# Edge counts built over 160 buckets of 16 nodes instead of 80 buckets of 32 nodes

## The reference, cut to what matters

```
x = x + L0_gnn(layernorm(x))     # twice: xW = x @ W[r]; agg = segment_sum(xW[edge_type, src], dst)
x = x + L0_ffn(layernorm(x))     # top 2 of 8 experts
x = x + L1_gnn(layernorm(x))     # three times: msg = h[src] * norm; agg = segment_sum(msg, dst)
x = x + L1_ffn(layernorm(x))     # top 2 of 8 experts
```

## Time and profile before

| | |
|---|---|
| median of three runs | 2288.94 us (2286.91 to 2291.53) |
| the profiled execution | 2287.31 us, its span 2285.4 us |
| busy, share of the span | PE 83%, DVE 53%, ACT 44%, POOL 41% |
| mean granted TensorE clock | 0.914 |
| first to last gather of `aggregate_and_gate` | 636.2 to 1075.6 us |
| last count product, last sum added | 1032.0 us, 1091.0 us |

### The profile page before, as it was taken

The page is one execution under the profiler, slowest core; times in us unless marked ns, Lnnn a source line. Parts: engine busy times, 40 slices in busy tenths (PEclk is TensorE's granted clock), DMA queues, the critical chain, the costliest instruction groups (busy, mean ns, idle before and its releaser), DMA issues. The chain is left out here.

```text
span 2285.4 us, 37277 instructions
## 1 busy us (share of the span) xinstructions
PE 1888.0 (83%) x10428; PEld 1570.3 (69%) x10428; DVE 1210.0 (53%) x2759; ACT 1002.6 (44%) x2229; POOL 934.0 (41%) x877
## 2 busy tenths in 40 slices
PE   5995688778848888787499999679899864999997
PEld 3873576656735555555489999558788854899996
DVE  6331222212268898793655555365554566666664
ACT  1555456546455656555033333245444421233332
POOL 0115777777367777776033433220000000333332
PEclk9997889989979999998599999879999965999998
DMA  4894666665368655564545342237664456424262
GB/s 153 344 363 175 223 219 213 226 224 207 127 206 320 215 199 193 197 206 150 207 124 160 90 123 42 63 133 251 235 218 173 166 223 248 121 42 123 43 191 41
DMA packets 127195, 410.00 MB, mean 179 GB/s; under 512 B 21012, under 2 KB 60928, under 8 KB 108544
## 3 DMA queue, kind: packets, MB, share of 16 engines
q1 hardware_dynamic: 56848, 185.62, 22.2%
q0 software_dynamic: 48096, 106.74, 18.2%
q10 hardware_dynamic: 22032, 114.96, 13.2%
HBM read 256.77 MB, written 150.47 MB: 178 GB/s over the span
## 5 line engine op out<-in xcount | busy, mean ns | idle before, releaser
L2231 PE MATMUL ps<-ring,halves 128*128 x3384 | 579.6, 326 | 11.8 <-SPq L2193 4.2
L2231 PEld LDWEIGHTS ps<-ring,halves 128*128 128x128 f32 x3384 | 487.2, 192 | 54.1 <-issue 13.5
L1429 POOL DMA_INDIRECT ring<-tab_rel_next,gidx_relation x313 | 345.2, 1103 | 137.6 <-issue 94.8
L1111 POOL DMA_INDIRECT relation_rest<-tab_rel,gidx_relation x313 | 309.9, 990 | 105.5 <-issue 94.8
L2340 ACT ACTIVATE x_all<-ps 128x512 f32<-128x512 f32 x188 | 113.0, 601 | 453.0 <-PE ps L2250 448.8
L1186 PE MATMUL ps<-relation_rest,slots 128*128 x784 | 210.5, 415 | 105.0 <-SPq L1026 103.7
L1521 PE MATMUL ps<-ring,slots 128*128 x784 | 205.2, 410 | 87.8 <-SPq L1306 46.3
L1888 PE MATMUL ps<-node_rows,blocks 128*128 128x512 f32 (+1 forms) x1200 | 258.8, 366 | 0.3 <-ACT blocks L1770 0.3
L1186 PEld LDWEIGHTS ps<-relation_rest,slots 128*128 128x128 f32 x784 | 157.8, 207 | 144.5 <-issue 119.3
L1521 PEld LDWEIGHTS ps<-ring,slots 128*128 128x128 f32 x784 | 151.1, 202 | 128.6 <-issue 108.3
L1888 PEld LDWEIGHTS ps<-node_rows,blocks 128*128 128x128 f32 x1200 | 203.3, 194 | 31.2 <-ACT blocks L1770 0.8
(11 more groups left out here) (281 smaller groups left out, 2773.9 us busy)
## 6 DMA issues: line engine op xcount, KB each, us to landing
ring<-split_weights SPq DMA_DIRECT2D x12, 4096.0 KB, 14.5
split_weights<-relation_rest ACTq DMA_DIRECT2D x32, 1024.0 KB, 7.4
slots<-tab_counts SPq DMA_DIRECT2D x40, 640.0 KB, 4.0
tab_rel<-relation_rest SPq DMA_DIRECT2D x20, 1024.0 KB, 5.8
tab_rel_next<-relation_rest ACTq DMA_DIRECT2D x20, 1024.0 KB, 4.2
relation_rest<-in_ffn_units ACTq DMA_DIRECT2D x16, 1024.0 KB, 5.5
ring<-split_weights SPq DMA_DIRECT2D x8, 2048.0 KB, 22.9
split_weights<-ring ACTq DMA_DIRECT2D x16, 1024.0 KB
```

The source lines that it names most:

```text
L1111: nc.gpsimd.indirect_dma_start(rows[:, s * wide:s * wide + D], None, table, bass.IndirectOffsetOnAxis(ap=gidx[:, t:t + 1], axis=0)).then_i ...
L1429: nc.gpsimd.indirect_dma_start(rows[:, s * D:(s + 1) * D], None, table, bass.IndirectOffsetOnAxis(ap=gidx[:, t:t + 1], axis=0)).then_inc(g ...
L2231: ins = nc.tensor.matmul(to, lhs[left], weights(slot, right, at, n), start=first and (left, right) == (0, 0), stop=last and left == 1)
```

## The change

Buckets are 16 nodes wide, so there are 160. Each takes four edge tiles, 20 x 16 = 320 places and so one PSUM bank: four buckets are in flight in the four banks. `pair_hots` has eight buffers, four for even and four for odd buckets, and the wait ahead of each is replaced by the one wait ahead of `src_hots` (for the bucket before last). `count_full` counts buckets, not edge tiles. All three engines do two buckets behind each of the first 80 groups. DVE makes two buckets ahead of the loop instead of one. Four small tensors used after the counts (`token_of_slot`, `place_of_slot`, `weight_of_slot`, `w_comb`) now lie within `count_key`, which is no longer needed then.

```
-NARROW = 32
+NARROW = 16
-WINDOW = 6
+WINDOW = 4
-HOTS = WINDOW
+HOTS = 2 * WINDOW
+COUNTBANKS = 4
...
-                step(v.tensor_single_scalar(part, raw[0], 5, ALU.arith_shift_right))
+                step(v.tensor_single_scalar(part, raw[0], 4, ALU.arith_shift_right))
...
-                    act.wait_ge(count_full, (k + 1) * WINDOW)
+                    act.wait_ge(count_full, k + 1)
...
-                    for g in range(2):
-                        to = strips[b % 2][:, g * (NPAD // 2):(g + 1) * (NPAD // 2)].rearrange("p (g c) -> p g c", c=P)
-                        nc.scalar.activation(to[:, :, q * NARROW:(q + 1) * NARROW],
-                                             self.ps[BANKS + k % 2 * 2 + g][:, 0:half].rearrange("p (g c) -> p g c", c=NARROW),
-                                             ACT.Copy).then_inc(bank_out, 1)
+                    to = strips[b % 2].rearrange("p (g c) -> p g c", c=P)
+                    nc.scalar.activation(to[:, :, q * NARROW:(q + 1) * NARROW],
+                                         self.ps[BANKS + k % COUNTBANKS][:, 0:KEYS].rearrange("p (g c) -> p g c", c=NARROW),
+                                         ACT.Copy).then_inc(bank_out, 1)
...
                     if k >= 2:
-                        dve.wait_ge(count_full, (k - 1) * WINDOW)
+                        dve.wait_ge(count_full, k - 1)
...
                     for j in range(WINDOW):
-                        if k:
-                            dve.wait_ge(count_full, (k - 1) * WINDOW + j + 1)
-                        v.tensor_scalar(pair_hots[j], places, base[:, k:k + 1], self.key[:, bass.ds(at + j, 1)],
+                        v.tensor_scalar(pair_hots[k % 2 * WINDOW + j], places, base[:, k:k + 1], self.key[:, bass.ds(at + j, 1)],
                                         ALU.add, ALU.is_equal).then_inc(pair_hot, 1)
...
                 count_hots(0)
+                count_hots(1)
...
-                    if g + 1 < NARROWS:
-                        count_hots(g + 1)
+                    if g + 1 < NARROWS // 2:
+                        count_hots(2 * g + 2)
+                        count_hots(2 * g + 3)
...
-                    if k >= 2:
-                        pe.wait_ge(bank_out, 2 * (k - 1))
+                    if k >= COUNTBANKS:
+                        pe.wait_ge(bank_out, k - COUNTBANKS + 1)
                     for j in range(WINDOW):
                         pe.wait_ge(pair_hot, k * WINDOW + j + 1)
-                        for h in range(2):
-                            last = t.matmul(self.ps[BANKS + k % 2 * 2 + h][:, 0:half], src_hots[k % 2][:, j * P:(j + 1) * P],
-                                            pair_hots[j][:, h * half:(h + 1) * half], start=(j == 0), stop=(j == WINDOW - 1))
-                        last.then_inc(count_full, 1)
+                        last = t.matmul(self.ps[BANKS + k % COUNTBANKS][:, 0:KEYS], src_hots[k % 2][:, j * P:(j + 1) * P],
+                                        pair_hots[k % 2 * WINDOW + j], start=(j == 0), stop=(j == WINDOW - 1))
+                    last.then_inc(count_full, 1)
```

More of the change, by code:

```diff
@@ L154, in __init__ @@
         self.r2, self.r3 = sb("root_of", [P, TILES]), sb("root", [P, TILES])
[L155 to L158, removed]
+        self.token, self.place = (self.key[:, k * MTILES:(k + 1) * MTILES].bitcast(U32) for k in range(2))
+        self.wslot = self.key[:, 2 * MTILES:3 * MTILES]
+        self.wcomb = self.key[:, 3 * MTILES:3 * MTILES + 2 * TILES]
         self.texp = sb("tile_expert", [1, MTILES + E], I32)
@@ L1347, in take_counts @@
                     b, q = k // PER, k % PER
-                    act.wait_ge(count_full, (k + 1) * WINDOW)
+                    act.wait_ge(count_full, k + 1)
                     if q == 0 and b >= 2:
                         act.wait_ge(strip_stored[b % 2], 16 * (b // 2))
-                    for g in range(2):
-                        to = strips[b % 2][:, g * (NPAD // 2):(g + 1) * (NPAD // 2)].rearrange("p (g c) -> p g c", c=P)
-                        nc.scalar.activation(to[:, :, q * NARROW:(q + 1) * NARROW],
-                                             self.ps[BANKS + k % 2 * 2 + g][:, 0:half].rearrange("p (g c) -> p g c", c=NARROW),
-                                             ACT.Copy).then_inc(bank_out, 1)
+                    to = strips[b % 2].rearrange("p (g c) -> p g c", c=P)
+                    nc.scalar.activation(to[:, :, q * NARROW:(q + 1) * NARROW],
+                                         self.ps[BANKS + k % COUNTBANKS][:, 0:KEYS].rearrange("p (g c) -> p g c", c=NARROW),
+                                         ACT.Copy).then_inc(bank_out, 1)
                     if q == PER - 1:
-                        act.wait_ge(bank_out, 2 * (k + 1))
+                        act.wait_ge(bank_out, k + 1)
                         act.dma_start(self.tab_counts[b], strips[b % 2]).then_inc(strip_stored[b % 2], 16)
@@ L1400, in _ @@
                         onehots(g + HOTROWS - 1)
-                    if g < NARROWS:
-                        take_counts(g)
+                    if g < NARROWS // 2:
+                        take_counts(2 * g)
+                        take_counts(2 * g + 1)
                     for after, work_on in ((0, row_root), (1, store_rows), (3, take_turned), (4, take_logits)):
@@ L1559, in _ @@
                             work_on(b)
-                    if g < NARROWS:
-                        count_products(g)
+                    if g < NARROWS // 2:
+                        count_products(2 * g)
+                        count_products(2 * g + 1)
     def gate_again(self):
```

## The result

The changed kernel takes 2301.33 us (median of five runs, 2298.28 to 2304.03) against 2288.94 us before (2286.91 to 2291.53): ratio 1.0049, 95% interval 1.0033 to 1.0065. It is **slower by half a per cent**, 12.4 us. The forecast of 2288.5 us is wrong, and the range ends 1.3 us under the result. The time is close to the one that the rival "DVE becomes the bound" gave, 2300.5 us. The profiled execution's span is 2299.3 us, 13.9 us longer than before.

The account below looks back on a forecast made before the run. The prediction took POOL's issuing of gathers to bound the counts stage. It summed -1 us in the stage and +0.6 at the start to -0.4, so 2288.94 became 2288.5 us, with a range of 2280 to 2300.

Parts of the forecast that it names:

- DVE becomes the bound: Rival: short comparisons stay at 0.356 us, DVE needs 406 of 380 us, +11 in the stage, 2300.5 us; chance 0.15.
- What bounds the kernel before: Counts stage, 636 to 1100 us: POOL's issuing of gathers sets the length, with 15 us of sums and norms behind.
- The port: Port shared by DVE and POOL: gathers held by DVE operations, -6 by chance, +8 and -3 from pairing, together -1 us.
- The pairing: A gather held by a group's first wide comparison makes its successor meet the second, held 0.44 us; second ones cost +8.
- upper end: Top of the gathers' term: pairing in full and each train meeting 17 us of gathers instead of 10, given as +5.
- Less stretched: Rival: gathers in the counts stage are held less, by chance alone or shorter holds; 2283.5 us or less; chance 0.27.
- a fuller port: Rival: pairing in full and gathers held by the comparison trains too, +5 + 0.6, 2294.5 us; chance 0.10.
- PE, ACT and the start: PE's 320 fewer count products gain nothing, ACT's work stays as before, and edge_layout at the start costs +0.6 us.
- The size of a short comparison: DVE's 320-column pair comparisons: 0.274 us each from start to start, against 0.356 for 640 columns.
- about 354 of 380 us are then busy: DVE, 650 to 1030 us: 31 us more work was set against 57.2 us of idle time.
- turning point: Length of a short comparison from which DVE as the bound would decide the time: 0.338 us a piece.
- POOL waiting for L1311: Sign that the prediction is wrong: POOL, which had no real wait, would wait for the ring, showing DVE as the bound.

Follow-up runs that it names:

- e4: Kernel before, with the column numbers for DVE's first comparison of each group read from PSUM instead of SBUF: 2267.57 us.
- e9: Kernel before, with each of the 480 pair comparisons of 640 columns made as two of 320: 2362.03 us.
- e2: Changed kernel, with the fourth pair comparison of each bucket left out from the third bucket on (counts wrong): 2276.41 us.
- e11: Changed kernel, with PE's register load for the next group's first edge tile moved ahead of the count products: 2296.39 us.
- e7: Changed kernel, with DVE's two register loads of the windows moved ahead of the group's sum: 2299.32 us.
- e10: Changed kernel, with three sets of one-hot buffers in place of two: 2303.03 us.
- e3: Changed kernel, with the last two count products of each bucket made twice, as many products as before (counts too large): 2307.8 us.
- e1: Kernel before, with one more DVE operation (bn_stats over 392 columns) ahead of each of 79 bucket builds: 2291.28 us.
- e8: Kernel before, with three more DVE operations (bn_stats over 256 columns) ahead of each later bucket build: 2297.7 us.
- e5: Changed kernel, with the same edit as e4 (column numbers read from PSUM): 2299.06 us.
- e12: e4 with each 2048-column weight difference, here and in the stage before, made in eight pieces of 256 columns: 2259.99 us.
- e13: e12 with PE's register load moved ahead of the count products as in e11: 2255.68 us.

## Why the prediction was wrong, step by step

- **What bounds the kernel before** was read rightly. e4 took 19 us off the gathers, and the stage followed in full.
- **The port.** Forecast -1 us for the gathers, measured -2.2. Sorted by the DVE operation in which each gather started, those that met L1454 were held 21 us before and 26 after (forecast 20 and 26), those at L1458 and L1456 12 and 3 (forecast 17 and 10), at L1447 12 and 15 (forecast 13 and 13). The pairing is real. The sum was near in part because errors cancelled, and its upper end was added up wrong: -1 and 7 more for the trains is +6, not +5. "Less stretched" and "a fuller port" both fall.
- **PE, ACT and the start.** 320 products fewer gained nothing, as forecast. Over the whole of the sums, the fp16 products' busy time fell from 159 to 136 us and that of the fp32 ones rose from 205 to 222, at a lower clock, which the prediction didn't expect. The start cost 0.4 us for the 0.6 forecast.
- **The first term that failed: a comparison's wait for a gather, put at nothing.** The size of a short comparison was forecast to a thousandth: 0.273 us from start to start in three steps of four, and in e9 as well. But the prediction let the port hold gathers only. In the kernel after, comparisons wait for gathers to end, and the mean is 0.29. These waits come to 10 us in the stage; without them, and with 2 us less in DVE's other operations, its busy time there would have grown by the forecast 31 or a little less, and not by 38.7. That the gather's last part holds the port against DVE is read off the times of the trace; no run tests it by itself.
- **The step that failed: "about 354 of 380 us are then busy", so POOL still sets the pace.** It set DVE's work against the whole length of the stage. DVE's waits from the first to the last count product, before:

```profile
DVE acc L1443 <- PE ps L1521: 21.9, 14, 5.9
DVE ring L1454 <- issue: 15.5, 31, 1.2
DVE ring L1454 <- PE ps L1532: 11.8, 23, 1.6
```

and after:

```profile
DVE ring L1454 <- issue: 18.9, 35, 1.5
DVE acc L1443 <- PE ps L1521: 11.5, 9, 2.8
DVE ring L1454 <- PE ps L1531: 8.0, 16, 1.2
```

  Of the 57.8 us that DVE idled in the stage, 27.3 stood ahead of L1454: a register load and a hand-over from PE that come back with the groups, behind which all the new work stands. They are still 26.9 in the kernel after. Free were some 30 us, under even the forecast's 31. The rival took its spare time from the same wrong place, 26 and 15 us, and so put the turning point at 0.338 us a piece. The kernel turned at 0.29. That its price came out right (+11 for +12.4) is in part luck.
- **From 38.7 us of work to 12.4 us of time.** Only 14.0 of the 38.7 us went into idle time: DVE idles 43.8 us in the stage, 57.8 before, and most of what it filled stood ahead of the sums (21.9 us, now 11.5). The other 24.7 us lengthened the stage. Behind the last count product the late sums catch up: 47.8 us to the last sum, 59.0 before, so 11.2 came back and 13.5 were left. Why 11.5 us of waits for sums stay is less certain. PE in its turn waits 22.1 us in the stage for DVE to free a bank (nothing before) and 22.4 for comparisons (14.0 before), so each engine waits for the other. Work taken from DVE helps clearly (e2), a register load moved ahead on PE or DVE by 8.1 and 4.1 us to the last sum (e11, e7, one profile each), a third buffer set by 1.6 (e10), and 320 more products on PE change nothing there (e3). I read this as a loop through both engines in which DVE has the larger part. How the 43.8 us of DVE's idling divide between its own register loads and PE's hand-over stays open: e7 moved the loads without removing them.
- **The chances.** "DVE as the bound" had 0.15. The prediction named what would show it, POOL waiting for L1311, and that row is there, with 9.2 us. SyncE's 303.0 us show it far more clearly. Three more of its signs failed: PE's wait for landings fell from 46.3 to 35.9 us instead of growing, DVE was busy for 340 of the same 380 us, not 354, and the last sum came at 1104.7, not within 3 us of 1091.5.

## What to carry to other kernels

An engine's idle time is spare only where the new work can stand in it: take off the waits that recur in every round (a register load, a hand-over) before setting added work against the rest. In e1 and e8 work that could stand in them cost little or nothing. Splitting work into more, smaller instructions can raise an engine's load even where it drops a third of the columns, so count instructions first. Where two engines share a port, ask what each loses to the other: here gathers were held 9 us less by the short comparisons, and the comparisons 10 us more by the gathers. When an engine shares a port with the one that sets the pace, look at where its operands lie before making its operations shorter: here that one line was worth 23 us, and the rearrangement -12.

## What the runs showed of the hardware

- **One operand in PSUM frees the port.** The comparison with two SBUF operands held gathers, 20.9 us in all; the same one with its column numbers in PSUM took as long (954 ns, 959 before) and held none of the 50 that started inside it (mean gather 1103 to 1043 ns, in the kernel after 1096 to 998). The Trainium skill, SBUF — State Buffer, "SBUF: two separate sides", names two SBUF inputs as what takes the shared pair; e4 agrees, by the opposite case.
- **A short DVE comparison has a fixed part of about 0.19 us**: 0.356 from start to start for 640 fp16 columns, 0.273 for 320 where no gather ends in the step. It is the same in e9 for the halves that have neither a semaphore nor a register instruction of their own. The Trainium skill, VectorE: DVE Perf Modes, "The TRN2 errata", gives 58 cycles and a quarter cycle per column, by which 0.144 us would be the estimate for 320; the trace has nearly twice that, and that page's own note says that the formula is too low for single operations.
- **A gather can hold a DVE comparison**: 110 of 480 steps of the 320-column comparison were longer than the usual 0.273 us, in 109 of them a gather ended, and 10 us went that way; in e9 it was 178 of 197 long steps and 26 us. Of the 640-column ones 4 of 400 were longer than 0.38 us. Why these aren't held as much stays open.
- **The granted clock fell when PE had less to do**: 0.96 with 960 count products in the stage, 0.90 with 640, and 0.96 again in e3 with 960. The other runs agree: 0.91 to 0.93 with 640 (e2, e5, e7, e10, e11), 0.96 to 0.99 with 960 (e1, e4, e8, e9, e12, e13). In the stage the products of the sums took 161.6 us at 0.96 and 181.9 at 0.90, so dropping a third of the count products (24 us) took only 2 us off PE's busy time.
